# Which engine sums which chunk of the softmax denominator

## The chip, the core and the metric

The program runs on one core of a Trainium2 chip. The core has TensorE (PE, matrix products into PSUM), VectorE (DVE), ScalarE (ACT), GpSimd (POOL), and the SyncE queue (SP), which starts transfers. Each engine works through its own instruction list in order, and waits on semaphores for the others. The metric is the device time of one launch in microseconds (us): the median of three runs of the kernel before is 5474.95 us (5473.14 to 5485.77).

## The reference

The program is one transformer layer over 4 sequences of 2048 tokens of width 512, with 16 heads of width 32:

```python
q, k_, v = ...                       # x @ W.T + b, 16 heads of 32
scores = einsum('bqhd,bkhd->bhqk', q, k_) * scale + bias   # three keys masked
attn   = softmax(scores, axis=-1)
ctx    = einsum('bhqk,bkhd->bqhd', attn, v)
y      = x + ctx @ Wo.T + bo         # then LayerNorm with gamma and beta
x      = layernorm(x + y_normed)
x      = layernorm(x + quantised_ffn(x))
```

The softmax needs, for each query and head, the sum of the exponentials over all 2048 keys: the denominator. The change is only about who adds it up.

## The kernel before

**Blocks.** The attention of one sequence is 4 groups of 4 heads times 4 tiles of 512 queries, so 16 blocks (`i`), and 64 blocks in all. A block goes through its 2048 keys in 16 chunks of 128 (`c`). After the 16 blocks of a sequence a token stage (`tokens`) does the output projection, the three norms and the feed-forward part.

**One chunk.** TensorE computes four score tiles for the next chunk (line 466), one for each head, keys on the partitions and queries along the row. ScalarE takes the exponential into the buffer `prob` (line 624), which has `NPB = 6` chunk buffers of 128 x 2048 numbers. TensorE multiplies them with the values into `ps_o` (line 491). Between the scores TensorE also computes "units" (line 451), 64 score tiles of the next block, whose row maxima VectorE takes (line 731): each block is prepared while the block before it runs. The units lie in chunks 1 to 13, about five in each.

**The maxima.** When all 64 units are reduced, VectorE runs a short chain: a reduce (line 733), a cast of 16 columns (735), a copy (737), and a subtraction with two SBUF inputs (738), the last two without a wait between them. TensorE then transposes the result (458), in chunk 14, behind the four scores of that chunk and ahead of the query projection (437), of the chunk's value product, and of all that remains of the block.

**The denominator.** A sum over keys is a sum over partitions. TensorE can make it by a product with a block of ones (`column_sums`, line 471, four head-wide products into `ps_z`), and does so for the chunks in `PE_SUMS`. For the other chunks (`POOL_SUMS`) GpSimd adds the chunk's exponentials elementwise into `acc` (line 906). With n chunks on its side it issues n - 1 additions of 128 x 2048, since the first adds two chunks. At the end of the block TensorE waits for the last addition (`padd`, line 498) and sums `acc` once. VectorE takes the reciprocal (744), and GpSimd scales and biases the context (890, 893) before its first addition of the next block.

**Buffers.** ScalarE may overwrite the buffer of a chunk when its reader is done. For chunk c this is the chunk c - 6; where that one is GpSimd's, the wait is for its addition (line 623). The first chunks of the next block wait for chunks 12 and 13 of this one.

**Key blocks.** In the blocks i = 0, 4, 8 and 12 TensorE first projects the keys and values of the next head group (lines 418, 426) while GpSimd has nothing to add.

Of the kernel before, what the change touches and what calls it, by code (L numbers as in the profile page):

```python
# [35 lines left out]
NBLK = NG * NQB  # L36
NSB, NMB = 3, 3

PE_SUMS = [2, 5, 8, 11, 14, 15]
POOL_SUMS = [c for c in range(NKC) if c not in PE_SUMS]  # L40
NADD = len(POOL_SUMS) - 1
ADD_OF = {c: max(i - 1, 0) for i, c in enumerate(POOL_SUMS)}
# [61 lines left out]
def build(nc, x, xT, wT, bqkv, woT, w_ffn, band, gamma, beta, bo, had, out):  # L104
# [3 lines left out]
    with ExitStack() as ctx:  # L108
# [298 lines left out]
        def _(pe):  # L407
# [61 lines left out]
            def column_sums(src, first, last):  # L469
                for h in range(HG):  # L470
                    mm = nc.tensor.matmul(ps_z[HD * h:HD * h + HD, :], ones[:, 0:HD], src[:, h, :], start=first, stop=last)  # L471
                return mm

            def attend(n, i):

                for c in range(NKC):
# [13 lines left out]
                    for h in range(HG):  # L490
                        mm = nc.tensor.matmul(ps_o[HD * h:HD * h + HD, :], vst[:, i // NQB % 2, c, HD * h:HD * h + HD],  # L491
                                              prob[:, c % NPB, h, :], start=c == 0, stop=c == NKC - 1)
                    if c in PE_SUMS:
                        if c == PE_SUMS[0]:
                            pe.wait_ge(zrec, n + 1)
                        mm = column_sums(prob[:, c % NPB], c == PE_SUMS[0], False)
                    mm.then_inc(pv, 1)
# [514 lines left out]
```

## Time and profile before

| | |
|---|---|
| median of three runs | 5474.95 us |
| the profiled execution's own time | 5483.18 us |
| its span, first to last instruction | 5481.3 us |
| TensorE busy | 5061.1 us, 92% |
| VectorE busy | 3425.7 us, 62% |
| GpSimd busy | 3130.0 us, 57% |
| ScalarE busy | 2601.1 us, 47% |
| granted TensorE clock, mean | 0.972 |
| GpSimd additions (line 906) | 576, of 4581 ns |

The profile names a group by line, engine, operation, and tiles written and read. Idle time is put down to what ended it. The engines overlap, so the busy times do not add up to the span: what a step is worth has to be read from who waits for it. Records of TensorE are pipelined and their lengths overlap; the distance between starts tells its pace.

### The profile page before, as it was taken

How to read it: one execution, taken by the hardware profiler on the slowest of the kernel's cores; microseconds unless marked ns; L12 is line 12 of the kernel's file. 1: busy time of each engine (PE TensorE's matmuls, PEld its weight loads, DVE VectorE, ACT ScalarE, POOL GpSimd, SP SyncE). 2: the span in 40 equal slices, each digit the busy share in tenths (PEclk: the TensorE clock that was granted, in tenths of full speed). 3: DMA queues.
4: the chain of work that ended last, by engine and by line, in shares of the span. 5: the costliest groups of instructions: out<-in, count | busy, mean ns of one | idle time of the engine just before them, and what ended most of it. 6: DMA issues, size and time to landing. Idle time of an engine off the chain costs nothing.

```text
span 5481.3 us, 91351 instructions
## 1 busy us (share of the span) xinstructions
PE 5061.1 (92%) x25289; PEld 2485.6 (45%) x25289; DVE 3425.7 (62%) x5960; ACT 2601.1 (47%) x4902; POOL 3130.0 (57%) x1103
## 2 busy tenths in 40 slices
PE   6999999998799999999879999999987999999987
PEld 3444444543444444444444444444444454444434
DVE  5575757566566665757657575666664756575757
ACT  0454545453454454545345454544544545454545
POOL 1564646566366665646636464666663656464655
PEclk7999999999899999999989999999998999999998
DMA  4414141323322314141331413223233231414122
GB/s 113 89 36 93 36 91 38 76 41 88 85 58 47 65 39 90 36 93 36 102 81 36 93 36 74 54 48 65 42 108 72 49 76 36 93 36 93 36 66 76
DMA packets 255631, 358.94 MB, mean 65 GB/s; under 512 B 17009, under 2 KB 104849, under 8 KB 255122
## 3 DMA queue, kind: packets, MB, share of 16 engines
q1 hardware_dynamic: 255122, 352.81, 28.9%
q8 instruction: 240, 3.93, 0.3%
q14 instruction: 269, 2.20, 0.1%
HBM read 212.67 MB, written 33.55 MB: 45 GB/s over the span
## 4 chain that ended last, share of the span: by engine, by line
PE 74%; DMA 10%; issue 5%; POOL 4%; DVE 2%; ACT 2%; SPq 1%; POOLq 0%; ACTq 0%; DVEq 0%
PE ps_m L451 21%; PE ps_s L466 19%; PE ps_o L491 16%; DMA qst<-lo 6%; PE ps_z L471 5%; PE ps_m L437 4%; PE ps_m L418 4%; PE ps_m L426 3%; DMA xk<-in_xT_dram 3%; PE ps_s L515 1%; SPq L284 1%; POOL prob L932 1%; POOL prob L936 1%; ACT prob L624 1%; POOL prob L921 1%
## 5 line engine op out<-in xcount | busy, mean ns | idle before, releaser
L731 DVE TENSOR_REDUCE umax<-ps_m 128x1 f32<-128x512 f32 x4160 | 2564.2, 683 | 711.8 <-PE ps_m L451 711.8
L624 ACT ACTIVATE prob<-ps_s 128x512 f32<-128x512 f32 x4096 | 2124.6, 601 | 1650.2 <-PE ps_s L466 1427.4
L906 POOL TENSOR_TENSOR acc<-acc,prob 128x2048 f32<-128x2048 f32 x512 | 2345.6, 4581 | 454.0 <-ACT prob L624 430.2
L466 PE MATMUL ps_s<-qst,kst 99*128 99x512 f32 x4096 | 1692.2, 428 | 130.7 <-ACT prob L624 76.6
L451 PE MATMUL ps_m<-kst,qst 97*128 97x512 f32 x4160 | 1724.7, 422 | 33.1 <-DMA qst<-lo 33.1
L466 PEld LDWEIGHTS ps_s<-qst,kst 99*128 99x128 f32 x4096 | 758.3, 189 | 1208.8 <-ACT prob L624 661.2
L491 PE MATMUL ps_o<-prob,vst 128*32 128x512 f32 x8192 | 1091.8, 605 | 0.0
L451 PEld LDWEIGHTS ps_m<-kst,qst 97*128 97x128 f32 x4160 | 791.7, 190 | 474.1 <-DVE umax L731 332.1
L906 POOL TENSOR_TENSOR acc<-prob 128x2048 f32<-128x2048 f32 x64 | 293.0, 4579 | 708.1 <-ACT prob L624 708.1
L890 POOL TENSOR_TENSOR obuf<-obuf,zinv 128x512 f32<-128x512 f32 x64 | 82.1, 1283 | 910.7 <-DVE zinv L744 910.7
L711 DVE SCALAR_TENSOR_TENSOR lo<-ps_m,bias,hi 128x512 fp32r<-128x512 f32 x134 | 100.6, 751 | 795.7 <-ACT hi L603 474.1
L744 DVE RECIPROCAL zinv<-ps_z 128x512 f32<-128x512 f32 x64 | 214.9, 3358 | 310.2 <-PE ps_z L471 310.2
L471 PE MATMUL ps_z<-prob,ones 128*32 128x512 f32 x3072 | 399.8, 592 | 0.0
L515 PE MATMUL ps_s<-vst,hi 128*128 128x512 f32 x512 | 239.8, 613 | 81.2 <-DMA hi<-ctxT_dram 81.2
L418 PE MATMUL ps_m<-xk,wkv 128*128 128x512 f32 x544 | 266.5, 636 | 50.9 <-DMA xk<-in_xT_dram 47.4
L491 PEld LDWEIGHTS ps_o<-prob,vst 128*32 128x32 f32 x8192 | 161.5, 108 | 291.1 <-issue 146.4
L426 PEld LDWEIGHTS ps_m<-wkv,xk 128*128 128x128 f32 x2176 | 253.7, 192 | 32.8 <-issue 32.8
L426 PE MATMUL ps_m<-wkv,xk 128*128 128x128 f32 x2176 | 253.9, 275 | 0.0
L437 PE MATMUL ps_m<-xq,wq 128*128 128x512 f32 x528 | 244.6, 606 | 0.7 <-issue 0.7
L603 ACT ACTIVATE hi<-ps_m,bias 128x512 fp32r<-128x512 f32 x68 | 46.7, 687 | 348.3 <-PE ps_m L418 175.4
L471 PEld LDWEIGHTS ps_z<-prob,ones 128*32 128x32 f32 x3072 | 99.8, 110 | 229.8 <-issue 229.8
L418 PEld LDWEIGHTS ps_m<-xk,wkv 128*128 128x128 f32 x544 | 104.4, 201 | 176.2 <-issue 172.5
(98 smaller groups left out, 2235.0 us busy)
## 6 DMA issues: line engine op xcount, KB each, us to landing
xk<-in_xT_dram SPq DMA_DIRECT2D x70, 1024.0 KB, 9.0
xq<-in_xT_dram SPq DMA_DIRECT2D x67, 1024.0 KB, 8.8
kst<-hi SPq DMA_DIRECT2D x136, 256.0 KB, 10.6
qst<-hi SPq DMA_DIRECT2D x132, 256.0 KB, 5.6
kst<-lo SPq DMA_DIRECT2D x68, 256.0 KB, 10.3
wq<-in_wT_dram SPq DMA_DIRECT2D x67, 256.0 KB, 9.2
qst<-lo SPq DMA_DIRECT2D x66, 256.0 KB, 6.8
ctxT_dram<-obuf SPq DMA_DIRECT2D x64, 256.0 KB, 2.5
```

Of the source, the lines that this page charges most:

```text
L418: mm = nc.tensor.matmul(ps_m[:, 0, :], wkv[:, 0, c], xk[:, t % 2, c], start=c == 0, stop=c == IC - 1)
L426: mm = nc.tensor.matmul(ps_m[:, 1, u * P:(u + 1) * P], xk[:, t % 2, c, u * P:(u + 1) * P], wkv[:, 1, c], start=c == 0, stop=c == IC - 1)
L437: mm = nc.tensor.matmul(ps_m[:, 0, :], wq[:, c], xq[:, c], start=c == 0, stop=c == IC - 1)
L451: nc.tensor.matmul(ps_m[:, u % NMB, :], qst[k % 2][0:RSTACK, h, qt * P:(qt + 1) * P], kst[k // NQB % 2][0:RSTACK, h, kb * QB:(kb + 1) * QB ...
L466: nc.tensor.matmul(ps_s[:, (i * HG * NKC + HG * c + h) % NSB, :], kst[i // NQB % 2][0:RALL, h, c * P:(c + 1) * P], qst[i % 2][0:RALL, h, : ...
L471: mm = nc.tensor.matmul(ps_z[HD * h:HD * h + HD, :], ones[:, 0:HD], src[:, h, :], start=first, stop=last)
L491: mm = nc.tensor.matmul(ps_o[HD * h:HD * h + HD, :], vst[:, i // NQB % 2, c, HD * h:HD * h + HD], prob[:, c % NPB, h, :], start=c == 0, st ...
L515: nc.tensor.matmul(ps_wo[t % 3], tC[t % 2][:, h * P:(h + 1) * P], wo_sb[:, h, :], start=h == 0, stop=False)
L624: nc.scalar.activation(prob[:, c % NPB, h, :], ps_s[:, (i * HG * NKC + HG * c + h) % NSB, :], ACT.Exp, scale=SCALE).then_inc(ex, 1)
L731: nc.vector.tensor_reduce(umax[:, m, kb:kb + 1], ps_m[:, u % NMB, :], AX.X, ALU.max).then_inc(mred, 1)
L744: nc.vector.reciprocal(zinv[:], ps_z[:]).then_inc(zrec, 1)
L906: nc.gpsimd.tensor_tensor(acc[:], a, prob[:, c % NPB], ALU.add).then_inc(padd, 1)
```

## The change

Chunks 2, 5, 8 and 11 go from TensorE to GpSimd, and chunk 7 goes from GpSimd to TensorE. The lists and the number of additions (`NADD`, 9 before and 12 after) are worked out from the one line.

```diff
-PE_SUMS = [2, 5, 8, 11, 14, 15]
+PE_SUMS = [7, 14, 15]
 POOL_SUMS = [c for c in range(NKC) if c not in PE_SUMS]
 NADD = len(POOL_SUMS) - 1
 ADD_OF = {c: max(i - 1, 0) for i, c in enumerate(POOL_SUMS)}
```

TensorE at the end of chunk 2 of a block, before (`ps_o` takes the value product, `ps_z` the denominator, `kst` and `qst` are the stacked keys and queries):

```order
L466 MATMUL ps_s<-qst0,kst0 128x512
L448 REGISTER_ALU
L451 MATMUL ps_m<-kst0,qst1 128x512
L448 REGISTER_ALU
L451 MATMUL ps_m<-kst0,qst1 128x512
L491 MATMUL ps_o<-prob,vst 32x512 x4
L471 MATMUL ps_z<-prob,ones 32x512 x4
L465 REGISTER_ALU
L466 MATMUL ps_s<-qst0,kst0 128x512
```

and the same place now:

```order
L466 MATMUL ps_s<-qst0,kst0 128x512
L448 REGISTER_ALU
L451 MATMUL ps_m<-kst0,qst1 128x512
L448 REGISTER_ALU
L451 MATMUL ps_m<-kst0,qst1 128x512
L491 MATMUL ps_o<-prob,vst 32x512 x4
L465 REGISTER_ALU
L466 MATMUL ps_s<-qst0,kst0 128x512
```

The four sums are gone there, as in chunks 5, 8 and 11; chunk 7 has gained four. GpSimd at the turn from one block to the next, where the first additions of a block stand behind the two steps on the context (the order there is the same before and now, but 9 additions follow before, and 12 now):

```order
L890 TENSOR_TENSOR obuf<-obuf,zinv 128x512 [waits zrec,oz_cp]
L893 TENSOR_SCALAR obuf<-obuf,bias 128x512 [waits cnorm]
L899 ISA
L906 TENSOR_TENSOR acc<-prob 128x2048 [waits zdone,ex]
L899 REGISTER_ALU
L904 ISA [waits ex]
L906 TENSOR_TENSOR acc<-acc,prob 128x2048 [waits padd]
```

Each addition waits for the exponentials of its chunk (`ex`) and for the addition before it (`padd`). On ScalarE some waits for a TensorE product (`pv`) become waits for a product and an addition, as here at the exponential of chunk 8, which writes over chunk 2:

```order
 L618 REGISTER_ALU
 L621 REGISTER_ALU [waits sc]
-L624 ACTIVATE prob<-ps_s 128x512 [waits pv]
+L623 REGISTER_ALU [waits pv]
+L624 ACTIVATE prob<-ps_s 128x512 [waits padd]
```

That exponential now waits for two engines instead of one. On VectorE and in the SyncE queue nothing is added, removed or moved.

## Rows read from the trace of the kernel before

**Rows 1.** The page: busy time, and the chain that ended last.

```profile
PE 5061.1 (92%) x25289; PEld 2485.6 (45%) x25289; DVE 3425.7 (62%) x5960; ACT 2601.1 (47%) x4902; POOL 3130.0 (57%) x1103
...
PE 74%; DMA 10%; issue 5%; POOL 4%; DVE 2%; ACT 2%; SPq 1%; POOLq 0%; ACTq 0%; DVEq 0%
```

**Rows 2.** Timeline of VectorE: start, length, instruction, idle before; two plain chunks, one with sums.

```profile
883.81 3.08 DVE L731 TENSOR_REDUCE umax<-ps_m 128x1 f32<-128x512 f32 x5 [0.44 <-PE ps_m L451]
887.35 3.08 DVE L731 TENSOR_REDUCE umax<-ps_m 128x1 f32<-128x512 f32 x5 [0.46 <-PE ps_m L451]
891.75 3.08 DVE L731 TENSOR_REDUCE umax<-ps_m 128x1 f32<-128x512 f32 x5 [1.32 <-PE ps_m L451]
```

**Rows 3.** Timeline of GpSimd in an ordinary block, and the next block's start.

```profile
819.42 1.30 POOL L890 TENSOR_TENSOR obuf<-obuf,zinv 128x512 f32<-128x512 f32 x1 [14.34 <-DVE zinv L744]
...
821.59 4.57 POOL L906 TENSOR_TENSOR acc<-prob 128x2048 f32<-128x2048 f32 x1
826.24 9.24 POOL L906 TENSOR_TENSOR acc<-acc,prob 128x2048 f32<-128x2048 f32 x2
...
864.50 4.59 POOL L906 TENSOR_TENSOR acc<-acc,prob 128x2048 f32<-128x2048 f32 x1
...
883.52 1.29 POOL L890 TENSOR_TENSOR obuf<-obuf,zinv 128x512 f32<-128x512 f32 x1 [14.42 <-DVE zinv L744]
```

**Rows 4.** Timeline, same block: last sum, reciprocal, next block's exponentials.

```profile
878.41 0.13 PEld L471 LDWEIGHTS ps_z<-acc,ones 128*32 128x32 f32 x4 [0.30 <-issue]
...
880.02 3.36 DVE L744 RECIPROCAL zinv<-ps_z 128x512 f32<-128x512 f32 x1 [4.96 <-PE ps_z L471]
...
876.02 2.06 ACT L624 ACTIVATE prob<-ps_s 128x512 f32<-128x512 f32 x4 [1.75 <-PE ps_s L466]
```

**Rows 5.** Timeline, same block, chunk 14: the maxima chain and TensorE behind it.

```profile
868.43 0.70 DVE L735 CAST mhi<-negm 128x16 fp32r<-128x16 f32 x1
869.16 0.17 DVE L737 COPY msplit<-mhi 128x16 f32<-128x16 f32 x1
869.25 0.17 DVE L738 TENSOR_TENSOR msplit<-negm,mhi 128x16 f32<-128x16 f32 x1
...
869.53 0.09 PEld L458 LDWEIGHTS ps_m<-ident,msplit 128*32 128x32 f32 x1
```

**Rows 6.** Line 735 in the whole run: ns minimum, median, maximum.

```profile
L735 DVE CAST mhi<-negm x65: 175/698/970, 125.9 to 5298.6; 128x16 fp32r<-128x16 f32 x65
```

**Rows 7.** Timeline of the setup: two GpSimd memsets in a row, a VectorE instruction.

```profile
6.95 14.77 POOL L959 MEMSET kst<- 3x8192 f32 x2
...
10.16 4.68 DVE L844 TENSOR_SCALAR qst<-vst 1x1024 fp32r<-1x1024 f32 x1
```

**Rows 8.** Timeline of the token stage: GpSimd beside a small VectorE product.

```profile
1323.15 1.30 POOL L936 TENSOR_TENSOR prob<-lo,acc 128x512 f32<-128x512 f32 x1
1323.34 1.12 DVE L778 TENSOR_TENSOR lnv<-lnv 128x1 f32<-128x1 f32 x1
1324.50 0.16 DVE L780 SCALAR_TENSOR_TENSOR lnv<-mv,lnv 128x1 f32<-128x1 f32 x1
```

**Rows 9.** Timeline of a key block (i = 4): first addition, cast of the maxima.

```profile
461.66 4.57 POOL L906 TENSOR_TENSOR acc<-prob 128x2048 f32<-128x2048 f32 x1 [29.07 <-ACT prob L624]
...
511.10 0.70 DVE L735 CAST mhi<-negm 128x16 fp32r<-128x16 f32 x1
```

**Rows 10.** Timeline of a sequence's last block: first addition, cast, reciprocal.

```profile
1238.15 4.59 POOL L906 TENSOR_TENSOR acc<-prob 128x2048 f32<-128x2048 f32 x1
...
1285.30 0.69 DVE L735 CAST mhi<-negm 128x16 fp32r<-128x16 f32 x1
...
1294.88 3.36 DVE L744 RECIPROCAL zinv<-ps_z 128x512 f32<-128x512 f32 x1 [3.06 <-PE ps_z L471]
```

**Rows 11.** Timeline of TensorE in a key block (i = 8): waits for transfers.

```profile
730.85 3.69 PE L418 MATMUL ps_m<-xk,wkv 128*128 128x512 f32 x8 [1.04 <-DMA xk<-in_xT_dram]
...
740.88 5.39 PE L418 MATMUL ps_m<-xk,wkv 128*128 128x512 f32 x8 [2.77 <-DMA xk<-in_xT_dram]
```

**Rows 12.** Stretches of key block i = 4, then an ordinary block: granted clock third last.

```profile
431.00:527.00 96.00, 90.83 (x485) 48.83 (x485) 48.17 (x75) 42.03 (x81) 43.51 (x12) 1.00 0.50 109
820.00:884.00 64.00, 62.66 (x322) 28.65 (x321) 44.65 (x71) 34.63 (x67) 43.10 (x12) 1.00 0.18 38
```

## The prediction, made before the changed kernel ran

> **What bounds the kernel now.** I read the page first: TensorE is busy 92% of the span and holds 74% of the chain that ended last, GpSimd is busy 57% [rows 1]. Then the timeline of one block, engine by engine. An ordinary block goes from one GpSimd scaling step to the next in 883.52 - 819.42 = 64.10 us [rows 3]. There are 44 such blocks, 4 that end a sequence, and 16 key blocks. VectorE's reductions follow TensorE's pace: 3.54 us for a chunk without denominator sums (887.35 - 883.81), 4.40 us for one with them (891.75 - 887.35) [rows 2]. So TensorE sets the pace, and one chunk's sums cost it 0.86 us. GpSimd adds at 4.65 us a chunk (821.59 to 826.24), of which 4.58 is the addition, and then waits 14.42 us for the end of the block [rows 3]. It has slack over a block, but an addition is slower than a TensorE chunk.
>
> **The change part by part.** *TensorE* loses the sums of four chunks and gains one: 3 x 0.86 = 2.58 us a block, 165 us in 64 blocks. That is the most the change can give, if nothing else is late.
>
> *GpSimd* gets 12 additions instead of 9. In the block of rows 3 the first starts at 821.59 and, since exponentials arrive every 3.5 to 4.4 us, they follow without a gap: the tenth ends at 821.59 + 9 x 4.65 + 4.58 = 868.02, the eleventh at 872.67, the twelfth at 877.32. Before, the last one ended at 864.50 + 4.59 = 869.09. The reciprocal starts 880.02 - 878.41 = 1.61 us after TensorE begins its last sum [rows 4]. No row shows TensorE waiting for an addition; I take 0.05 us for the signal, so the reciprocal can't start before 878.98. It started at 880.02: GpSimd alone leaves a gain of 1.04 us of the 2.58. GpSimd becomes the second bound.
>
> *Buffers.* The tightest is the next block's chunk 0, which needs the eleventh addition (872.67). Its exponentials started at 876.02 [rows 4], so 873.44 with the earlier pace: no wait, by 0.8 us. The longer queue of GpSimd reaches ScalarE nowhere else. The wait for `zrec` moves from chunk 2 to chunk 7 and costs nothing, since the reciprocal is long done.
>
> *The maxima chain.* This is what decides. The cast of 16 columns starts at 868.43 and takes 0.70 us [rows 5], against 0.175 us where GpSimd is idle [rows 6]. It ends at 869.13, which is 0.04 us after GpSimd's last addition (869.09) [rows 3, 5]. The median of 65 casts is 0.698 us [rows 6], so it is so in nearly every block. The small product with two SBUF inputs in the token stage does the same: 1.12 us, ending at 1324.46 when the GpSimd instruction beside it ends at 1324.45; the next one, with GpSimd idle, takes 0.16 [rows 8]. So such a VectorE instruction that meets a running GpSimd instruction waits until it ends. The copy (line 737) is of the cast's kind, the subtraction (738) of the product's kind. Today the addition that they meet is the last of the block, so they wait for it once and all three pass. TensorE's transpose follows 0.11 us later, at 869.53, with no more than that to spare.
>
> After the change the cast is ready at 868.43 - 2.58 = 865.85, in the tenth addition (863.44 to 868.02), with two more behind it. The setup shows what happens between two: a VectorE instruction starting at 10.16 in the first of two memsets ends at 14.84; the first memset ends at 6.95 + 7.35 = 14.30, half of the pair's 14.77 less the gap [rows 7]. So the waiting instruction is let in between two GpSimd instructions, which stand some 0.07 us apart. The cast then ends at 868.05. The copy would start 0.03 us later, the subtraction 0.09 us after it [rows 5], at 868.17; the eleventh addition is due at 868.09. No row shows a second and third VectorE instruction there with GpSimd waiting too. Bounds: all three pass together (transpose at 868.45, 1.08 us earlier than before), or each waits for one more addition (the last passes at 877.34, transpose at 877.45, 7.92 later). I take the middle: one of the copy and the subtraction gets in, the other waits for the eleventh addition and passes at 872.69. The copy starts before the addition, but the subtraction is dispatched after the addition is due. Transpose at 872.80, 3.27 us later than before. Behind the transpose stand the query projection, two value products, three sums and the next scores, and nothing of it can pass: the end of the block moves by the same 3.27, and the next one starts from there. 44 x 3.27 = 144 us.
>
> *Last blocks.* First addition 1238.15, eleventh ends at 1289.23, transpose at 1289.36 against 1285.30 + 1.10 = 1286.40 [rows 10]: 4 x 3.0 = 12 us.
>
> *Key blocks.* Here the first addition starts with chunk 1, GpSimd is late from nothing. In i = 4: first addition 461.66, cast ready at 511.10 - 2.58 = 508.52 [rows 9]. The eleventh addition runs from 508.16 to 512.74, so the cast just misses the gap, and the second instruction waits for the twelfth: 517.39, transpose 517.52 against 512.20, 5.3 us later. 16 x 5.3 = 85 us.
>
> *Clock.* TensorE would stand still before the transpose from 869.53 - 2.58 = 866.95 to 872.80, 5.9 us a block. In key block i = 8 eight products that take 3.69 us took 5.39 after a 2.77 us wait, and 3.69 after 1.04 us [rows 11]; block i = 4, which also waits for its loads, kept a granted clock of 1.00, and so does an ordinary block now [rows 12]. A clock that falls to its lower level costs 5.39 - 3.69 = 1.7 us each time. Bounds: 0 and 64 x 1.7 = 109 us. A wait twice as long as the one that cost it speaks for the upper end; I take two blocks in three, 73 us.
>
> **Sum.** 144 + 12 + 85 + 73 = 314 us. The profiled execution took 5483.18 us (span 5481.3, 1.9 around it) and would take 5797. It is 8.2 us above the median, so the forecast is 5789 us.
>
> The Trainium skill, "SBUF — State Buffer", section "Who interferes with whom", says that VectorE in a two-port mode (copy and cast can enter it) or with two SBUF inputs shares a port pair with GpSimd, and that who issues first has it for the whole instruction while the other fully blocks. The trace agrees on one such wait [rows 5, 8]. The section does not say who gets the pair when both stand waiting. Read strictly, each of the three instructions would wait on its own; that is the third case below.
>
> **The rivals.**
>
> *All three pass in one gap (GpSimd-bound).* For it: the copy starts before GpSimd's next instruction is due, and the subtraction is only 0.09 us behind. Then an ordinary block ends with GpSimd, 1.04 us earlier, or 0.8 if the addition is held up by the 0.24 us of the three: 44 x 0.9 = 40 us gained. The last block loses: twelfth addition ends at 1293.88, reciprocal at 1295.54 plus up to 0.24 against 1294.88, 4 x 0.8 = 3. A key block has its cast at 512.74, transpose at 513.17 against 512.20: 16 x 0.97 = 15 lost. Sum -22 us: 5453. The key blocks miss the gap by 0.36 us; were they to hit it, they would gain up to 2.58 each, 57 us in all against this sum: 5396. This case lies on the edge between faster and no change.
>
> *Each of the three waits for its own addition.* Ordinary 44 x 7.92 = 348, last blocks 1293.88 + 0.13 - 1286.40 = 7.6, x 4 = 30, key blocks 85, since there is no addition after the twelfth. With 463 us and one or two falls of the clock per block (64 x 1.7 to 3.4): 6050 to 6160. Against it: the copy starts 0.03 us behind the cast, ahead of the addition.
>
> *TensorE alone decides.* If GpSimd's additions neither held the chain nor ended late, the whole 165 us would come: 5310. The arithmetic of the twelve additions speaks against it.
>
> **How the numbers follow.** The middle case 0.42, all three in one gap 0.38, each on its own 0.14, TensorE alone or something else on the faster side 0.04, others 0.02. The middle case's own range is 5690 (no fall of the clock, some blocks that hit a gap) to 5850 (a fall in every block). No change is within 0.3%, 16 us, about what a measurement of this kernel can tell. The second case, at -22 with some 25 either way, splits into 0.20 faster, 0.17 no change, 0.01 slower. Faster: 0.20 + 0.04 = 0.24. No change: 0.18. Slower: 0.42 + 0.14 + 0.02 = 0.58. The range that holds 8 in 10 has to take in both: 5440 to 5850, and it leaves out the third case.
>
> **What would show it.** In the changed kernel's profile: 768 additions, 4.65 us apart, twelve in a row. The cast of line 735 at a median of about 2.2 us. Either line 737 or 738 at a median near 4.6 us: then this forecast holds; both near 0.17: the second case; both long: the third. TensorE idle before line 458 by about 5.9 us, blocks of 67.4 us or, with the clock, up to 69.1. In the second case TensorE would wait instead before its last sum for line 906, and blocks would be 63.1 to 63.4 us. The forecast is wrong if VectorE's three instructions stay short, or if the additions stretch beyond 4.65 us.

## The result, and the profile after

The changed kernel takes 5835.45 us (median of 4 runs, 5827.89 to 5844.38) against 5476.61 us for the kernel before on the same chip (4 runs, 5473.14 to 5485.77). The ratio is 1.0653 [1.0633, 1.0673]: slower by 359 us. The forecast was 5789, 46 us less, with a range that ended at 5850.

The page of the changed kernel: busy time, the chain that ended last, and three groups (busy time, mean ns of one, idle time before them and what ended it).

```profile
PE 5023.4 (86%) x23721; PEld 2481.2 (43%) x23753; DVE 3824.7 (66%) x5960; ACT 2600.2 (45%) x4902; POOL 3999.9 (69%) x1295
...
PE 65%; DVE 12%; DMA 10%; issue 6%; POOL 4%; ACT 1%; SPq 1%; POOLq 0%; DVEq 0%; ACTq 0%
...
L437 PE MATMUL ps_m<-xq,wq 128*128 128x512 f32 x528 | 371.8, 869 | 0.8 <-issue 0.7
L458 PE MATMUL ps_m<-ident,msplit 128*32 128x128 f32 x65 | 24.2, 372 | 387.8 <-DVE msplit L738 387.8
...
L738 DVE TENSOR_TENSOR msplit<-negm,mhi 128x16 f32<-128x16 f32 x65 | 286.5, 4407 | 0.0
```

The trace holds 1568 records of TensorE products fewer, and TensorE is busy 38 us less than in [rows 1], and yet the span grew by 345. The line to stop at is the one of L458: TensorE stands idle 387.8 us in 65 waits, 6.0 us each on average, for VectorE's subtraction of 16 columns. That subtraction now takes 4407 ns on average, and VectorE's share of the chain rose from 2% [rows 1] to 12%.

The three instructions of the maxima chain in the whole run, changed kernel (ns minimum, median, maximum):

```profile
L735 DVE CAST mhi<-negm x65: 174/2252/4484, 125.6 to 5636.5; 128x16 fp32r<-128x16 f32 x65
```

```profile
L737 DVE COPY msplit<-mhi x65: 174/174/176, 125.8 to 5638.0; 128x16 f32<-128x16 f32 x65
```

```profile
L738 DVE TENSOR_TENSOR msplit<-negm,mhi x65: 166/4473/4475, 125.9 to 5638.1; 128x16 f32<-128x16 f32 x65
```

Now one ordinary block in the timeline, GpSimd first; it is the answer to [rows 3].

```profile
865.96 1.29 POOL L890 TENSOR_TENSOR obuf<-obuf,zinv 128x512 f32<-128x512 f32 x1 [16.17 <-DVE zinv L744]
...
868.12 4.57 POOL L906 TENSOR_TENSOR acc<-prob 128x2048 f32<-128x2048 f32 x1
872.77 51.02 POOL L906 TENSOR_TENSOR acc<-acc,prob 128x2048 f32<-128x2048 f32 x11
934.80 1.29 POOL L890 TENSOR_TENSOR obuf<-obuf,zinv 128x512 f32<-128x512 f32 x1 [11.01 <-DVE zinv L744]
```

The same block, VectorE and TensorE at the maxima chain; it is the answer to [rows 5].

```profile
912.40 2.25 DVE L735 CAST mhi<-negm 128x16 fp32r<-128x16 f32 x1
914.68 0.17 DVE L737 COPY msplit<-mhi 128x16 f32<-128x16 f32 x1
914.76 4.47 DVE L738 TENSOR_TENSOR msplit<-negm,mhi 128x16 f32<-128x16 f32 x1
...
919.38 0.37 PE L458 MATMUL ps_m<-ident,msplit 128*32 128x128 f32 x1 [5.63 <-DVE msplit L738]
919.61 5.21 PE L437 MATMUL ps_m<-xq,wq 128*128 128x512 f32 x8
```

The tenth and the eleventh addition of that block, each by itself:

```profile
910.04 4.57 POOL L906 TENSOR_TENSOR acc<-acc,prob 128x2048 f32<-128x2048 f32 x1
...
914.69 4.51 POOL L906 TENSOR_TENSOR acc<-acc,prob 128x2048 f32<-128x2048 f32 x1
```

Twelve additions in a row take 872.77 + 51.02 - 868.12 = 55.67 us, 4.65 from start to start. The tenth ends at 914.61, and the next one begins 0.08 us later. In that gap the waiting cast completes (914.65) and the copy starts, 0.01 us before the eleventh addition does, and it passes; the subtraction starts 0.07 us into the eleventh addition and ends 0.03 us behind it, at 919.24. TensorE has stood still for 5.63 us by then. The eight products behind the transpose take 5.21 us, and 3.67 in the same place of the kernel before. The block is 934.80 - 865.96 = 68.84 us long, against 64.10 [rows 3]. GpSimd still waits 11.01 us at its end: it is not what bounds the block.

The clock in the stretch of one block (us, then busy time of TensorE, its weight loads, VectorE, ScalarE and GpSimd; the granted clock is third last), and in the few us around the wait:

```profile
868.00:937.00 69.00, 62.03 (x302) 28.67 (x305) 50.74 (x72) 34.74 (x68) 56.91 (x16) 0.95 0.17 36
...
917.00:921.00 4.00, 1.61 (x3) 0.93 (x4) 2.24 (x1) 1.21 (x3) 3.92 (x2) 0.50 0.01 2
```

The clock was 1.00 over the whole block before [rows 12]. Now it is 0.50 of 2.4 GHz, the level of 1.2 GHz, when TensorE takes up work after the standstill, and 0.95 over the block. In all 64 blocks the eight products of line 437 are longer than before: 4.96 us in the mildest block, 6.64 in the worst, against 3.67 in all 64 before.

### The profile page after: what moved, and what is told of

The parts are those of the page before. It is cut to its first block, busy times and chain, and to the rows that moved or that the text cites. A ratio compares the mean times of both kernels' runs of the same rounds, so it can differ in the third digit from the quotient of the medians.

```text
span 5826.1 us, 89015 instructions
## 1 busy us (share of the span) xinstructions
PE 5023.4 (86%) x23721; PEld 2481.2 (43%) x23753; DVE 3824.7 (66%) x5960; ACT 2600.2 (45%) x4902; POOL 3999.9 (69%) x1295
## 4 chain that ended last, share of the span: by engine, by line
PE 65%; DVE 12%; DMA 10%; issue 6%; POOL 4%; ACT 1%; SPq 1%; POOLq 0%; DVEq 0%; ACTq 0%
PE ps_m L451 19%; PE ps_s L466 16%; PE ps_o L491 14%; PE ps_m L437 6%; DMA qst<-lo 6%; DVE msplit L738 5%; PE ps_m L418 3%; PE ps_m L426 3%; DVE mhi L735 3%; DMA xk<-in_xT_dram 3%; DVE umax L731 2%; PE ps_z L471 2%; POOL prob L932 1%; POOL prob L936 1%; SPq L284 1%
## 5 line engine op out<-in xcount | busy, mean ns | idle before, releaser
L906 POOL TENSOR_TENSOR acc<-acc,prob 128x2048 f32<-128x2048 f32 x704 | 3215.6, 4568 | 55.2
L890 POOL TENSOR_TENSOR obuf<-obuf,zinv 128x512 f32<-128x512 f32 x64 | 82.1, 1283 | 800.7 <-DVE zinv L744 800.7
L437 PE MATMUL ps_m<-xq,wq 128*128 128x512 f32 x528 | 371.8, 869 | 0.8 <-issue 0.7
L458 PE MATMUL ps_m<-ident,msplit 128*32 128x128 f32 x65 | 24.2, 372 | 387.8 <-DVE msplit L738 387.8
L738 DVE TENSOR_TENSOR msplit<-negm,mhi 128x16 f32<-128x16 f32 x65 | 286.5, 4407 | 0.0
L614 ACT ACTIVATE mrow<-ps_m 32x128 fp32r<-32x128 f32 x65 | 17.3, 266 | 470.5 <-PE ps_m L458 470.5
L437 PEld LDWEIGHTS ps_m<-xq,wq 128*128 128x128 f32 x528 | 146.1, 292 | 179.4 <-issue 172.0
```

What stands on the lines that cost most here:

```text
L437: mm = nc.tensor.matmul(ps_m[:, 0, :], wq[:, c], xq[:, c], start=c == 0, stop=c == IC - 1)
L738: nc.vector.tensor_tensor(msplit[:, HG * NQB:], negm[:], mhi[:].bitcast(F32), ALU.subtract).then_inc(mneg, 1)
L906: nc.gpsimd.tensor_tensor(acc[:], a, prob[:, c % NPB], ALU.add).then_inc(padd, 1)
```

## The experiments

All ratios are against the kernel before on the same chip, with 95% intervals. "The block" is the time from one L890 to the next, as a mean over the 44 ordinary blocks: 64.21 us before, 69.46 in the changed kernel.

### The place in the chain, or the kind of instruction?

The change, with the subtraction ahead of the copy:

```diff
-                nc.vector.tensor_copy(msplit[:, 0:HG * NQB], mhi[:].bitcast(F32))
-                nc.vector.tensor_tensor(msplit[:, HG * NQB:], negm[:], mhi[:].bitcast(F32), ALU.subtract).then_inc(mneg, 1)
+                nc.vector.tensor_tensor(msplit[:, HG * NQB:], negm[:], mhi[:].bitcast(F32), ALU.subtract)
+                nc.vector.tensor_copy(msplit[:, 0:HG * NQB], mhi[:].bitcast(F32)).then_inc(mneg, 1)
```

> The changed kernel with the subtraction (738) put ahead of the copy (737), both behind the cast. Theory (place decides: after the cast one more VectorE instruction gets in before GpSimd's next addition, the one behind it waits for that whole addition): the subtraction is now short, about 0.17 us, the copy takes about 4.47 us, TensorE waits 5.6 us before the transpose as before, and the time stays at 5835 us, within 10. Rival (kind decides: only the instruction with two SBUF inputs is kept out): the subtraction stays at about 4.5 us although it comes first, and the copy behind it is short. Second rival (free once the cast is through): both short, 5455 us.

Measured: 5835.03 us, ratio 1.0650 [1.0632, 1.0668]. The timeline of this kernel in one block:

```profile
908.13 2.35 DVE L735 CAST mhi<-negm 128x16 fp32r<-128x16 f32 x1
910.52 0.17 DVE L737 TENSOR_TENSOR msplit<-negm,mhi 128x16 f32<-128x16 f32 x1
910.61 4.47 DVE L738 COPY msplit<-mhi 128x16 f32<-128x16 f32 x1
...
915.23 0.37 PE L458 MATMUL ps_m<-ident,msplit 128*32 128x128 f32 x1 [5.75 <-DVE msplit L738]
```

In 63 of 64 blocks the long one is now the copy (median 4472 ns, the subtraction's 176), and the time is the same. So the kind of instruction does not decide. In the remaining block, the first, the chain began at another moment:

```profile
217.00 0.17 DVE L735 CAST mhi<-negm 128x16 fp32r<-128x16 f32 x1
217.21 4.37 DVE L737 TENSOR_TENSOR msplit<-negm,mhi 128x16 f32<-128x16 f32 x1
221.50 0.16 DVE L738 COPY msplit<-mhi 128x16 f32<-128x16 f32 x1
...
217.01 4.53 POOL L906 TENSOR_TENSOR acc<-acc,prob 128x2048 f32<-128x2048 f32 x1
```

The cast started 0.01 us before an addition and passed at once; the subtraction, second in the chain, started 0.2 us into that addition and waited for it; the third was short. So it is not the place in the chain either, but whether an instruction starts before or after GpSimd's next one. The traces of the change, of this kernel and of the one with spare products below agree, in all 64 blocks of each: what started before the next addition, though by only 3 to 15 ns, took under 0.18 us, and what started behind its start, by 31 ns or more, waited for its end.

### Taking GpSimd out of the maxima chain

The reduce writes into an unused part of the accumulator memory (PSUM), the cast reads it there and writes straight into `msplit`, the copy is gone, and the subtraction has one input in PSUM and one in SBUF. First in the changed kernel:

```diff
-                nc.vector.tensor_reduce(negm[:], umax[:], AX.X, ALU.max, negate=True).then_inc(mstep, 1)
+                negp = ps_m[:, 2, 0:HG * NQB]
+                nc.vector.tensor_reduce(negp, umax[:], AX.X, ALU.max, negate=True).then_inc(mstep, 1)
...
-                nc.vector.tensor_copy(mhi[:], negm[:]).then_inc(mstep, 1)
+                nc.vector.tensor_copy(msplit[:, 0:HG * NQB].bitcast(F32R), negp).then_inc(mstep, 1)
...
-                nc.vector.tensor_copy(msplit[:, 0:HG * NQB], mhi[:].bitcast(F32))
-                nc.vector.tensor_tensor(msplit[:, HG * NQB:], negm[:], mhi[:].bitcast(F32), ALU.subtract).then_inc(mneg, 1)
+                nc.vector.tensor_tensor(msplit[:, HG * NQB:], negp, msplit[:, 0:HG * NQB], ALU.subtract).then_inc(mneg, 1)
```

> The changed kernel with the negated maxima written to PSUM, so that cast and subtraction have at most one SBUF operand to read, and the copy gone (the cast writes where the copy wrote). Theory (the loss is the wait of these instructions for GpSimd and what follows from it): no instruction of the chain is over 0.2 us, TensorE no longer waits before the transpose, the clock stays up; ordinary blocks become GpSimd's, 1.04 us shorter than in the kernel before (46 us in all), key blocks TensorE's, 2.58 us shorter (41 us), last blocks 0.7 longer (3 us): 5392 us. Rival (the added GpSimd work costs by itself, through buffers or slower access for the others): over 5700 us.

Measured: 5368.48 us, ratio 0.9792 [0.9776, 0.9809]. The cast and the subtraction of this kernel in the whole run:

```profile
L736 DVE CAST msplit<-ps_m x65: 174/175/177, 127.2 to 5179.5; 128x16 fp32r<-128x16 f32 x65
```

```profile
L738 DVE TENSOR_TENSOR msplit<-ps_m,msplit x65: 174/174/177, 127.4 to 5179.8; 128x16 f32<-128x16 f32 x65
```

In all 64 blocks both start while an addition runs, and neither is ever longer than 0.18 us. The whole loss is gone: 467 us less than the change as it was made. The end of a block shows what bounds it now:

```profile
2169.47 1.07 PE L471 MATMUL ps_z<-acc,ones 128*32 128x512 f32 x8 [1.12 <-POOL acc L906]
2170.67 3.36 DVE L744 RECIPROCAL zinv<-ps_z 128x512 f32<-128x512 f32 x1 [6.29 <-PE ps_z L471]
...
2174.18 1.29 POOL L890 TENSOR_TENSOR obuf<-obuf,zinv 128x512 f32<-128x512 f32 x1 [4.76 <-DVE zinv L744]
```

TensorE waits for the last addition, the reciprocal follows, then the scaling, and GpSimd is idle only for these 4.76 us. The block is 62.67 us, set by GpSimd, as the arithmetic of the twelve additions said; it is 0.4 us shorter than that arithmetic gave, and the kernel 24 us faster than expected, mostly because the reciprocal starts 1.20 us after the last sum's start and not the 1.61 of [rows 4].

TensorE stands still here too, for 1.0 to 1.6 us before the last sum, in each of the 44 ordinary blocks, and behind none of these waits did the clock fall.

The same edit in the kernel before tells what the chain costs there.

> The kernel before with the maxima chain through PSUM as in the other experiment. Theory: in the kernel before the cast's wait of 0.5 us ends before TensorE is ready for the transpose, so nothing is gained: 5476 us within 8, though the cast falls from 0.70 to about 0.2 us. Rival (the chain is on the path already): 0.5 to 0.6 us a block, 5440 us.

Measured: 5469.3 us, ratio 0.9981 [0.9972, 0.9991], some 10 us. The cast falls from 0.698 us [rows 6] to 0.175 and the time hardly moves: the waits of the kernel before lay almost wholly beside TensorE's work. So the 467 us belong to the change and the chain together, not to the chain alone.

### The clock by itself

The change, with six spare products of 128 x 512 on TensorE in the time in which it would wait. The transpose writes over their result, and nothing reads it:

```diff
+                if not first:
+                    pe.wait_ge(mred, (f + 1) * UNITS)
+                    for _ in range(FILL):
+                        nc.tensor.matmul(ps_m[:, 1, :], ident[:], wscale[:], start=True, stop=True)
                 pe.wait_ge(mneg, f + 1)
```

> The changed kernel with six products of 128x128 by 128x512 in TensorE's list ahead of its wait for the maxima; their result is written over by the transpose. They take about 6 x 0.9 = 5.4 us and lie in the 5.6 us in which TensorE stood still. Theory (part of the loss is the clock that falls after the standstill): granted clock 1.00 in ordinary blocks, query projection back at 3.67 us, time 5476 + 241 = 5717 us. Rival (the standstill alone costs, the clock is a bystander): 5835 us, or more by what the products overrun.

Measured: 5710.57 us, ratio 1.0422 [1.0404, 1.0439], 125 us less than without them. A block's stretch of this kernel, and the products of line 437 (here 438) in it:

```profile
900.00:967.00 67.00, 65.25 (x310) 30.15 (x309) 50.63 (x70) 34.44 (x67) 56.58 (x15) 1.00 0.17 37
```

```profile
899.52 3.67 PE L438 MATMUL ps_m<-xq,wq 128*128 128x512 f32 x8
```

The transpose is as late as before, and the ordinary block is 67.25 us: 3.04 more than before, which is the price of the late transpose alone. The clock is back at 1.00 in this block, and the products are at 3.67 us in all ordinary ones. In the key blocks the spare products are done too early, TensorE still stands for 1.0 to 2.6 us, and in 9 of the 16 the eight products took 5.15 to 5.37 us. So the spare products gave back most of what the clock had cost, not all: 125 us, 2.0 in each block. The products of that line in the whole run take 258.3 us:

```profile
L438 PE MATMUL ps_m<-xq,wq 128*128 128x512 f32 x528 | 258.3, 635 | 0.9 <-issue 0.7
```

### One more addition on GpSimd in the kernel before

The kernel before, with a spare addition of 128 x 512 as GpSimd's last instruction of a block:

```diff
                     nc.gpsimd.tensor_tensor(acc[:], a, prob[:, c % NPB], ALU.add).then_inc(padd, 1)
+                nc.gpsimd.tensor_tensor(spare[:], wscale[:], wscale[:], ALU.add)
```

> The kernel before with one more GpSimd addition of 128x512 (about 1.29 us) behind the last addition of each block, into a spare tile that nobody reads or waits for. Theory (an instruction that GpSimd has standing ready gets in behind the copy, and the subtraction waits for it): the subtraction takes about 1.2 us instead of 0.17, the transpose comes 1.0 us later, the wait is too short for the clock to fall: 5476 + 64 = 5540 us. Rival (only the amount of denominator work on either engine matters): 5476 us, since GpSimd idles 14 us there.

Measured: 5530.29 us, ratio 1.0095 [1.0078, 1.0112], 53 us more. The time came out, the detail did not. The timeline of this kernel:

```profile
874.08 0.69 DVE L736 CAST mhi<-negm 128x16 fp32r<-128x16 f32 x1
874.70 1.03 POOL L908 TENSOR_TENSOR spare<-wscale 128x512 f32<-128x512 f32 x1
874.81 0.96 DVE L738 COPY msplit<-mhi 128x16 f32<-128x16 f32 x1
875.69 0.16 DVE L739 TENSOR_TENSOR msplit<-negm,mhi 128x16 f32<-128x16 f32 x1
```

Here the copy waits (median 962 ns), the second of the chain, and the subtraction goes with it. The spare addition waits for no semaphore and starts at 874.70, before the cast has ended; between two additions of the block, each of which waits for the semaphore `padd`, the next starts 0.07 us after the end of the last. So here the copy starts 0.1 us behind GpSimd's next instruction, where in the change it started 0.01 us ahead of it, and it waits. That the spare addition comes so early because it waits for nothing is my reading.

### Ten or eleven additions

Two lists that leave GpSimd less (line 40):

```diff
-PE_SUMS = [7, 14, 15]
+PE_SUMS = [3, 6, 10, 14, 15]
```

> The kernel before with sums of chunks 3, 6, 10, 14, 15 on TensorE: 10 additions. Theory (what counts is whether an addition stands behind the one that the cast meets): the last addition ends 52.1 us after the reciprocal's start, the cast is ready at 51.65 and waits for that one alone, all three instructions pass: 0.86 us less in every block, 5476 - 55 = 5421 us. Rival (the loss grows with the number of additions, a third of 359 us for one of three): 5596 us.

Measured: 5495.29 us, ratio 1.0032 [1.0021, 1.0044]. This was a miss by 74 us. The timeline of one block of this kernel:

```profile
2254.80 13.91 POOL L906 TENSOR_TENSOR acc<-acc,prob 128x2048 f32<-128x2048 f32 x3 [1.14 <-ACT prob L624]
...
2269.17 0.27 PE L458 MATMUL ps_m<-ident,msplit 128*32 128x128 f32 x1 [0.68 <-DVE msplit L738]
2269.39 5.37 PE L437 MATMUL ps_m<-xq,wq 128*128 128x512 f32 x8
```

The chain meets the last addition and passes in one, as expected (the cast's median is 1804 ns, the other two are short). But the additions do not run without gaps: GpSimd waited 1.14 us for the exponentials of a chunk, so the last addition ended later than I had worked out, and TensorE waited 0.68 us. Over the run it waits 57.3 us for line 738, in 65 waits, which is most of the miss. In 9 of 64 blocks the clock fell too, as here, with 5.37 us for the eight products; a wait of 0.83 us in the block before it left them at 3.67.

```diff
-PE_SUMS = [7, 14, 15]
+PE_SUMS = [5, 10, 14, 15]
```

> The kernel before with sums of chunks 5, 10, 14, 15 on TensorE: 11 additions. Theory: in ordinary and last blocks the cast is ready in the tenth addition and the eleventh stands behind it, so the subtraction waits for the eleventh and the transpose comes 3.27 us late, as in the changed kernel, with TensorE still for 5.0 us and a clock fall of about 2 us; in key blocks the cast meets the last addition, 1.0 us late. 48 x 5.3 + 16 x 1.0 = 270: 5746 us. Rival (loss by the number of additions, two thirds of 359): 5715 us, but with key blocks as slow as the others. Rival (nothing at stake but TensorE's sums): 5366 us.

Measured: 5776.8 us, ratio 1.0549 [1.0531, 1.0566]. The timeline of an ordinary block of this kernel:

```profile
1209.88 1.55 DVE L735 CAST mhi<-negm 128x16 fp32r<-128x16 f32 x1
1211.46 0.18 DVE L737 COPY msplit<-mhi 128x16 f32<-128x16 f32 x1
1211.55 4.47 DVE L738 TENSOR_TENSOR msplit<-negm,mhi 128x16 f32<-128x16 f32 x1
```

One addition less, and an ordinary block is no shorter (69.46 us): the chain still meets an addition that has another behind it. The key blocks are 99.8 us against 102.9, since there the cast meets the last one and the subtraction is short. What counts is how many additions stand behind the one that the chain meets, not how many there are. The time is 31 us above the 5746 expected: a key block costs 2.9 us more than before and not 1.0, for TensorE still stands there for 1.3 to 2.8 us, and in 13 of 16 the clock fell.

The list of eleven with the chain through PSUM:

> The same 11 additions with the maxima chain through PSUM. Theory: TensorE sets the pace in every block and GpSimd's end lies 4 us before it is needed: 64 x 1.72 = 110 us less than the kernel before, 5366 us, which is also less than with 12 additions, where GpSimd sets the pace. Rival (GpSimd's end comes into the way here too): near 5392 us.

Measured: 5371.57 us, ratio 0.9803 [0.9786, 0.9819]. With the chain free, eleven and twelve additions take the same time within these intervals. I had expected eleven to be the faster; the ordinary block is indeed shorter (62.32 against 62.67 us), but the key blocks are longer (96.3 against 94.1), and no run shows why.

### Two instructions in the chain instead of three

The change, with the cast writing into `msplit` and the copy gone; the subtraction keeps its two SBUF inputs:

```diff
-                nc.vector.tensor_copy(mhi[:], negm[:]).then_inc(mstep, 1)
+                nc.vector.tensor_copy(msplit[:, 0:HG * NQB].bitcast(F32R), negm[:]).then_inc(mstep, 1)
...
-                nc.vector.tensor_copy(msplit[:, 0:HG * NQB], mhi[:].bitcast(F32))
-                nc.vector.tensor_tensor(msplit[:, HG * NQB:], negm[:], mhi[:].bitcast(F32), ALU.subtract).then_inc(mneg, 1)
+                nc.vector.tensor_tensor(msplit[:, HG * NQB:], negm[:], msplit[:, 0:HG * NQB], ALU.subtract).then_inc(mneg, 1)
```

> The changed kernel with the copy taken out: the cast writes straight into the tile that the copy filled, and the subtraction, still with two SBUF inputs, comes next. Theory (the cast and one more instruction get in between two additions, a third does not): cast 2.25 us as in the changed kernel, subtraction 0.17 instead of 4.47, TensorE waits for it at most 1.5 us; ordinary blocks about 63 us, key blocks 1 us longer than in the kernel before: 5440 us if the clock stays up, 5476 us if it falls in one block of three as in the experiment with ten additions. Rival (the instruction with two SBUF inputs is kept out whatever its place): 5835 us.

Measured: 5519.31 us, ratio 1.0076 [1.0059, 1.0093]. The timeline of this kernel:

```profile
934.87 2.27 DVE L735 CAST msplit<-negm 128x16 fp32r<-128x16 f32 x1
937.18 0.17 DVE L737 TENSOR_TENSOR msplit<-negm,msplit 128x16 f32<-128x16 f32 x1
...
937.50 0.27 PE L458 MATMUL ps_m<-ident,msplit 128*32 128x128 f32 x1 [1.26 <-DVE msplit L737]
937.72 5.37 PE L437 MATMUL ps_m<-xq,wq 128*128 128x512 f32 x8
```

Both pass in one gap in each of the 64 blocks (the subtraction's maximum is 176 ns). Against the change 316 us are won back by taking out one copy of 16 columns. It is still 38 us slower than before: TensorE waits 1.26 us for the tenth addition in an ordinary block and up to 3.5 in a key block (101.5 us in 65 waits), and in 46 of 64 blocks the eight products behind the wait are partly at the lower clock. I had expected the clock to stay up (5440) or to fall at an average price (5476), and both were too low.

### Versions that beat both

The kernel before with one line changed, so that GpSimd's last addition is that of chunk 12 and there are ten:

```diff
-PE_SUMS = [2, 5, 8, 11, 14, 15]
+PE_SUMS = [4, 8, 13, 14, 15]
```

> The kernel before with sums of chunks 4, 8, 13, 14, 15 on TensorE: 10 additions, GpSimd's last one is chunk 12's. Theory (the earlier attempt with 10 additions lost because its last addition started 1.3 us late, waiting for the exponentials of chunk 11 and 12): now the last addition ends 46.4 us after the first one starts, the cast is ready at 45.1 and done by 46.5, the transpose is not held up, since TensorE reaches it at 47.1: 0.86 us less a block, 5422 us. Rival (any cast wait over 1 us costs, by the clock or the chain): 5476 to 5500 us.

Measured: 5401.72 us, ratio 0.9854 [0.9837, 0.9870]. The chain of this kernel:

```profile
913.24 1.33 DVE L735 CAST mhi<-negm 128x16 fp32r<-128x16 f32 x1
914.61 0.17 DVE L737 COPY msplit<-mhi 128x16 f32<-128x16 f32 x1
914.69 0.17 DVE L738 TENSOR_TENSOR msplit<-negm,mhi 128x16 f32<-128x16 f32 x1
```

The cast still meets an addition, but it is the last, and no wait of TensorE for line 738 is left. The block is 63.17 us.

The change with the chain through PSUM, and with GpSimd's first addition of a block put ahead of the scaling of the block before (except in key blocks):

```diff
                     nc.gpsimd.tensor_tensor(acc[:], a, prob[:, c % NPB], ALU.add).then_inc(padd, 1)
+                    if k == 0 and between is not None:
+                        between()
...
-                        if i > 0:
+                        if i > 0 and i % NQB == 0:
                             normalise(n - 1, i - 1)
-                        attend(n)
+                        attend(n, (lambda: normalise(n - 1, i - 1)) if i % NQB else None)
```

> The changed kernel with the maxima chain through PSUM, and with GpSimd's first addition of a block put ahead of the scaling of the context of the block before (in all but key blocks). Theory (with the chain out of the way the block is GpSimd's at 62.7 us, since its first addition waits for reciprocal and scaling, 5.7 us): the first addition starts 2.6 us after the reciprocal's start, GpSimd's end comes 3 us earlier, TensorE and GpSimd end together at 61.5 to 61.7 us a block; key blocks as in the kernel with 12 additions and the chain through PSUM. 48 x 1.0 = 48 us less than that kernel's 5368: 5322 us. Rival (something else holds the block at 62.2 to 62.7): 5345 to 5368 us.

Measured: 5315.11 us, ratio 0.9702 [0.9685, 0.9718], the fastest of all. GpSimd and the last sum in one block of this kernel:

```profile
909.45 4.59 POOL L906 TENSOR_TENSOR acc<-prob 128x2048 f32<-128x2048 f32 x1 [3.97 <-ACT prob L624]
913.99 1.28 POOL L890 TENSOR_TENSOR obuf<-obuf,zinv 128x512 f32<-128x512 f32 x1
...
916.14 51.09 POOL L906 TENSOR_TENSOR acc<-acc,prob 128x2048 f32<-128x2048 f32 x11
967.29 1.06 PE L471 MATMUL ps_z<-acc,ones 128*32 128x512 f32 x8 [0.66 <-POOL acc L906]
```

The reciprocal's time now lies under the first addition. That is 166 us less than the kernel before on the same chip (5481.25). It is near the 165 that three sums a block are worth on TensorE, in part by chance: some 10 of the 166 are what the chain through PSUM gives in the kernel before as well, and TensorE still waits 0.66 us in the block shown.

## Why the prediction was right

**The mechanism held, in each step.** The additions are 4.65 us apart, twelve in a row without a gap. The cast takes 2.25 us in the median, predicted 2.2. The third instruction of the chain takes 4.47, predicted 4.5. TensorE stands idle 5.63 us in the block shown, 7.7 in a key block and 6.0 on average, predicted 5.9. I had said that the third waits because it is dispatched after the addition is due, and not because of its kind. The swap shows both, the second by its 63 blocks and the first by the one block in which the second instruction came late and waited. That the chain is the whole cause, and not the exponentials or the buffers, is shown by the version through PSUM, which leaves all twelve additions and every buffer as they are and loses nothing. This stood at 0.42 against 0.38 for the case in which all three pass, on one pair of memsets [rows 7]; the removed copy shows that case was one instruction away. I had the copy 0.01 us ahead of the eleventh addition, and it starts 6 to 14 ns ahead of it: that so thin a margin held in every block was luck as well as arithmetic.

**The waits, 241 us, were a little too high.** With the spare products the change costs 5710.57 - 5710.57 / 1.0422 = 231 us. Some 14 of these are still clock, in the key blocks: the products of line 437 take 258.3 us there and 244.6 in the kernel before. That leaves 217. An ordinary block pays 3.04 us (predicted 3.27), a last one 65.32 - 62.44 = 2.9 (3.0), and a key block 102.02 - 96.98 = 5.0 with its share of the clock (5.3 without).

**The clock, 73 us, was the term that was mis-sized.** It cost the 125 us that the spare products gave back and the 14 that they did not, some 139. The products of line 437 by themselves take 371.8 us in the changed kernel, and in the kernel before

```profile
L437 PE MATMUL ps_m<-xq,wq 128*128 128x512 f32 x528 | 244.6, 606 | 0.7 <-issue 0.7
```

which is 127 us, so most of it falls on the eight products behind the wait. Two things were off. I let the clock fall in two blocks of three; it fell in all 64. And I priced a fall at 1.7 us, from one block in which the clock was low for only part of the eight products [rows 11]: it was 1.00 from 740.9 to 741.9 us, 0.50 from 742.9 to 744.9, and 1.00 again from 745.9. In the changed kernel a fall costs these products 1.3 us (4.96 us long) to 3.0 (6.64), 2.0 on average; over those of 6.64 us the granted clock is 0.54. The upper bound of 109 us was too low for the same reason. My own sentence had it, that a wait twice as long as the one that cost something speaks for the upper end, and I took the middle. 66 us more for the clock and 24 less for the waits make 42 of the 46 by which the forecast was short.

**The same error stood in the rivals.** I priced the case in which all pass without any clock, at 5453. The kernel without the copy is that case, made real, and takes 5519: the transpose is earlier there, but TensorE arrives earlier still, and behind its wait of 1.26 us the clock falls in most blocks. A wait of 1.04 us had cost nothing and one of 2.77 had [rows 11]; the runs here have falls after 0.68 and 1.26 and none after 0.83, and none after the 1.0 to 1.6 us before the last sum in the version through PSUM, so the length of the wait alone does not tell which block loses. "TensorE alone", 5310, fell by the arithmetic of the additions, as I had said, but with the chain free and the first addition early its number was reached to 5 us.

**The rule on the shared port.** The chain's lengths show who blocks whom: with its inputs in SBUF the third instruction takes 4.47 us, and with a PSUM input the same subtraction takes 0.174 beside the same additions. The Trainium skill, "SBUF — State Buffer", section "Who interferes with whom", says that a VectorE instruction with at most one SBUF input, outside the two-port modes, does not contend with GpSimd. By that rule the edit had to free the chain, and the trace agrees in all 64 blocks. The section's other sentence, that the first to issue has the pair and the other fully blocks, gave my third case as I read it; the traces agree with it if it is taken for each pair of instructions, since one that starts in the gap, before GpSimd's next, is then the first.

**Left open.** No run made the gap before a waiting addition wider, or set the chain's start on purpose; that the order of starts decides is read from the starts as they fell. Why the clock falls behind some short waits of TensorE and not behind others stays open. The spare addition changes two things at once, its missing wait and its length. That it starts earlier since it waits for no semaphore is my reading of the timeline, not shown by a run of its own.

## What to carry to other kernels

When work is moved to an engine that shares something with another, look for the small instructions of the other engine that today meet the last piece of it, and ask what they meet once there is another piece behind. Price every new standstill of TensorE twice, for the wait and for the clock of the work behind it, and take the clock's full price in each block unless a row shows a standstill of that length, at that place, that cost nothing. If a short chain decides, change the chain before changing how the work is split: the same split went from 6.5% slower to 2% faster with the chain's operands in PSUM and one copy out of it. The copy alone gave 316 of these 467 us.

## What the runs showed of the hardware that was not expected

Two VectorE instructions that cannot run beside GpSimd's additions get through between two of them 0.08 us apart: the one that was waiting, and one that starts behind it, 6 to 15 ns before the next addition. The third, 70 ns or more into that addition, waits for the whole of it (4.47 us). This was so in all 64 blocks of the change, and in 63 with copy and subtraction swapped. Before a GpSimd instruction that waits for no semaphore only the cast got through; there the copy started 0.1 us behind it.

Short standstills of TensorE can cost clock, and their length does not tell which do. With 1.6 us on average before the transpose (101.5 / 65) the clock fell in 46 of 64 blocks, and the next eight products then mostly took 5.37 us instead of 3.67; with 0.9 on average (57.3 / 65) it fell in 9. With 1.0 to 1.6 us before the block's last sum, in the version through PSUM, it fell behind none of 44. Six products whose result nothing reads, put into the wait, kept the eight products at 3.67 us in every ordinary block, though in only 7 of 16 key blocks, and took 125 us off the kernel.
